# Placing the tiles of a saturated matmul kernel in SBUF by their address modulo 128 bytes

## The reference

```python
def _L0_gnn_ref(input_graph, adj, Wq, bq, Wk, bk, Wv, bv, beta):   # 12 heads of 32
    q, k, v = (_split_heads(input_graph @ W + b) for each of the three)
    scores = jnp.einsum('bhqd,bhkd->bhqk', q, k) / sqrt(32) + beta * adj_e
    scores = jnp.where(adj_e > 0, scores, -9e15)
    return merge_heads(jnp.einsum('bhqk,bhkd->bhqd', jax.nn.softmax(scores, -1), v))
# _L1_gnn_ref: two layers, each
    a = jax.nn.softmax(jnp.einsum('bid,bjd->bij', h, h) / sqrt(384), axis=-1)
    delta = a * adjacency_matrix
    attn = delta / (jnp.sum(delta, axis=-1, keepdims=True) + 1e-10)
    hl, hs, hr = h @ wl.T + b_l, h @ ws.T + b_s, h @ wr.T + b_r
    ctx = (attn * upper) @ hl + diag(attn)[..., None] * hs + (attn * lower) @ hr
    h = relu(layernorm(ctx) * g + beta)
x = _layernorm(x + _L0_gnn_ref(x, adj, ...), axis=-1)
x = _layernorm(x + _L1_gnn_ref(x, adj, ...), axis=-1)
```

## The kernel before

| | function | moving | stationary | columns moved | matmuls per step |
|---|---|---|---|---|---|
| H | `project_sides`, `project_self` | `w_hi`, `w_lo` | `hT_hi`, `hT_lo` | 384 | 108 |
| A | `mix` | `hlr_hi`, `hlr_lo` | `aT_hi`, `aT_lo` | 386 | 24 |
| V | `project_v` | `w_hi`, `w_lo` | `xT_hi`, `xT_lo` | 384 | 18 |
| Q | `project_qk` | `xT_hi`, `xT_lo` | `w_hi`, `w_lo` | 256 | 54 |

## Time and profile before

### The profile page before, as it was taken

One profiled execution on the slowest core, in us unless ns is written; L12 is line 12 of the kernel. 1 busy time (PEld: TensorE's weight loads), 2 busy tenths in 40 slices (PEclk: granted clock), 3 DMA queues, 4 the chain that ended last, 5 costly groups with the idle time before them and its releaser, 6 DMA issues.

```text
span 1405.7 us, 37486 instructions
## 1 busy us (share of the span) xinstructions
PE 1345.0 (96%) x13568; PEld 1321.4 (94%) x13568; DVE 1085.8 (77%) x2665; ACT 755.5 (54%) x1579; POOL 597.0 (42%) x656
## 2 busy tenths in 40 slices
PE   3799999999999999999999999999999999999894
PEld 3799999999999999999999999999999999999894
DVE  3358887878887888887787888788888778787765
ACT  4355555564555555555555555555555555555453
POOL 1334444444444444444444445444444444444432
PEclk9799999999999999999999999999999999999997
DMA  7210111110011111011111011111001111101000
GB/s 239 77 39 8 44 50 51 50 49 20 29 49 49 49 49 36 12 49 49 49 49 49 14 35 49 49 49 49 25 24 49 49 49 49 49 2 40 24 13 23
DMA packets 49445, 62.74 MB, mean 45 GB/s; under 512 B 14320, under 2 KB 35952, under 8 KB 49392
## 3 DMA queue, kind: packets, MB, share of 16 engines
q1 hardware_dynamic: 49392, 62.03, 14.4%
HBM read 36.44 MB, written 12.58 MB: 35 GB/s over the span
## 4 chain that ended last, share of the span: by engine, by line
PE 95%; DMA 2%; DVE 1%; issue 1%; ACT 1%; POOL 0%; SPq 0%; POOLq 0%; ACTq 0%
PE bank L315 26%; PE bank L317 25%; PE bank L316 25%; PE bank L392 5%; PE bank L426 4%; PE bank L378 3%; PE bank L364 3%; PE bank L413 2%; PE bank L403 2%; DMA late<-in_w 2%; PE bank L454 1%; ACT w_hi L519 0%; DVE ln_six L840 0%; DVE w_lo L682 0%; ACT late L620 0%
## 5 line engine op out<-in xcount | busy, mean ns | idle before, releaser
L315 PE MATMUL bank<-w_hi,hT_hi 128*128 128x384 f32 x1152 | 402.9, 350 | 4.5 <-issue 3.6
L316 PE MATMUL bank<-w_lo,hT_hi 128*128 128x384 f32 x1152 | 390.7, 339 | 0.0
L317 PE MATMUL bank<-w_hi,hT_lo 128*128 128x384 f32 x1152 | 390.7, 339 | 0.0
L996 POOL TENSOR_TENSOR hlr_lo<-late,hlr_hi 128x384 fp32r<-128x384 f32 x256 | 239.5, 941 | 264.9 <-ACT hlr_hi L595 263.1
L595 ACT ACTIVATE hlr_hi<-late 128x384 fp32r<-128x384 f32 x256 | 134.3, 524 | 212.2 <-DVE late L797 210.3
L315 PEld LDWEIGHTS bank<-w_hi,hT_hi 128*128 128x128 f32 x1152 | 216.9, 188 | 10.1 <-issue 5.7
L316 PEld LDWEIGHTS bank<-w_lo,hT_hi 128*128 128x128 f32 x1152 | 217.4, 189 | 0.0
L317 PEld LDWEIGHTS bank<-w_hi,hT_lo 128*128 128x128 f32 x1152 | 217.0, 188 | 0.0
L797 DVE TENSOR_TENSOR late<-bank,rows 128x384 f32<-128x384 f32 x256 | 141.9, 554 | 89.2 <-PE bank L317 88.5
L1009 POOL TENSOR_TENSOR ln_rstd<-ln_var,minus_half 128x2 f32<-128x2 f32 x128 | 98.9, 772 | 225.0 <-DVE ln_var L866 117.3
L315 PE MATMUL bank<-xT_hi,w_hi 128*128 128x256 f32 x576 | 164.6, 286 | 9.1 <-ACT kT L534 9.1
(11 more groups left out here) (93 smaller groups left out, 2903.2 us busy)
## 6 DMA issues: line engine op xcount, KB each, us to landing
v_halves<-v_stage SPq DMA_DIRECT2D x128, 99.0 KB, 2.3
xT_in<-in_xT SPq DMA_DIRECT2D x32, 384.0 KB, 3.2
x_in<-in_x SPq DMA_DIRECT2D x32, 384.0 KB, 3.9
out<-late SPq DMA_DIRECT2D x32, 384.0 KB, 2.4
late<-in_w SPq DMA_DIRECT2D x9, 576.0 KB, 6.2
adj_in<-in_adj SPq DMA_DIRECT2D x32, 64.0 KB, 3.6
adjT_in<-in_adjT SPq DMA_DIRECT2D x64, 32.0 KB, 2.9
rows<-in_bl SPq DMA_DIRECT2D x2, 192.0 KB, 6.2
```

Of the source, the lines that this page charges most:

```text
L315: nc.tensor.matmul(o, l_hi, r_hi, start=n == 0, stop=False)
L316: nc.tensor.matmul(o, l_hi, r_lo, start=False, stop=False)
L317: done = nc.tensor.matmul(o, l_lo, r_hi, start=False, stop=n == last)
L996: nc.gpsimd.tensor_tensor(hlr_lo[:, t, m, 0:D], hlr[:, t, m], hlr_hi[:, t, m, 0:D].bitcast(F32), ALU.subtract).then_inc(hlrlo_ready, 1)
```

## The change

The change moves tiles within SBUF and pads one kind of row. All that moves through TensorE in a large product with the weights or in `mix`, and `kT`, `ident` and `v_halves`, now starts at a multiple of 128 bytes. After `v_halves` (6336 bytes, 49.5 x 128) come the tiles that are stationary, 64 bytes behind a multiple. The small tiles that TensorE doesn't read come last. The row of `hlr_hi` and `hlr_lo` is allocated 416 floats long (`MPAD`, 1664 bytes, 13 x 128) in place of 386; the matmul still moves 386 of them. Engine for engine, every instruction, its shape, its waits and its place in the order are the same in both kernels.

```diff
+MPAD = 416
@@
         w_hi = sb("w_hi", [P, NW, KC, D], F32R)
         w_lo = sb("w_lo", [P, NW, KC, D], F32R)
+        kT = sb("kT", [P, KC, TOK])
+        ident = sb("ident", [P, P])
+        hlr_hi = sb("hlr_hi", [P, T, 2, MPAD], F32R)
+        hlr_lo = sb("hlr_lo", [P, T, 2, MPAD], F32R)
         rows = sb("rows", [P, 9, D])
-        bq_col, bk_col = sb("bq_col", [P, KC]), sb("bk_col", [P, KC])
...
+        v_halves = sb("v_halves", [P, T, GRAPHS, H * VW])
         xT_hi = sb("xT_hi", [P, KC, TOK], F32R)
         xT_lo = sb("xT_lo", [P, KC, TOK], F32R)
-        qT, kT = sb("qT", [P, KC, TOK]), sb("kT", [P, KC, TOK])
-        v_stage = sb("v_stage", [P, T, H, VW])
-        v_halves = sb("v_halves", [P, T, GRAPHS, H * VW])
...
+        qT = sb("qT", [P, KC, TOK])
+        pT = sb("pT", [P, T * PAIRS, P])
         probs = sb("probs", [P, T, HC, 2, 2, N])
...
-        hlr_hi = sb("hlr_hi", [P, T, 2, MW], F32R)
-        hlr_lo = sb("hlr_lo", [P, T, 2, MW], F32R)
...
+        bq_col, bk_col = sb("bq_col", [P, KC]), sb("bk_col", [P, KC])
...
                     product(CTX_BANKS[t][:, 0:MW],
-                            [((aT_hi[:, t, m, :], aT_lo[:, t, m, :]), (hlr_hi[:, t, m, :], hlr_lo[:, t, m, :]))
+                            [((aT_hi[:, t, m, :], aT_lo[:, t, m, :]), (hlr_hi[:, t, m, 0:MW], hlr_lo[:, t, m, 0:MW]))
```

More of the change, by code:

```diff
@@ L127, in resnorm_kernel @@
         adj_diag = sb("adj_diag", [P, 2, T, N])
+        v_halves = sb("v_halves", [P, T, GRAPHS, H * VW])
         xT_hi = sb("xT_hi", [P, KC, TOK], F32R)
         xT_lo = sb("xT_lo", [P, KC, TOK], F32R)
-        qT, kT = sb("qT", [P, KC, TOK]), sb("kT", [P, KC, TOK])
-        v_stage = sb("v_stage", [P, T, H, VW])
-        v_halves = sb("v_halves", [P, T, GRAPHS, H * VW])
-        score_mask = sb("score_mask", [P, T, N])
-        score_add = sb("score_add", [P, T, N])
+        qT = sb("qT", [P, KC, TOK])
+        pT = sb("pT", [P, T * PAIRS, P])
         probs = sb("probs", [P, T, HC, 2, 2, N])
-        row_max = sb("row_max", [P, T * H])
-        pT = sb("pT", [P, T * PAIRS, P])
-        r_sum = sb("r_sum", [P, T, H])
         h0 = sb("h0", [P, 2, T, D])
@@ L146, in resnorm_kernel @@
         hT_lo = sb("hT_lo", [P, T, KC, P], F32R)
-        u_max, u_bias = sb("u_max", [P, T]), sb("u_bias", [P, T])
         e_di = sb("e_di", [P, T, 2, N])
-        z_di = sb("z_di", [P, T])
-        diag_junk = sb("diag_junk", [P, T, N])
-        diag, dz, den, den_sq = sb("diag", [P, T]), sb("dz", [P, T]), sb("den", [P, 2, T]), sb("den_sq", [P, 2, T])
-        hlr_hi = sb("hlr_hi", [P, T, 2, MW], F32R)
-        hlr_lo = sb("hlr_lo", [P, T, 2, MW], F32R)
         aT = sb("aT", [P, T, 2, P])
@@ L166, in resnorm_kernel @@
                  for r in range(RAW)]
+        bq_col, bk_col = sb("bq_col", [P, KC]), sb("bk_col", [P, KC])
+        g0_col, b0_col = sb("g0_col", [P, KC]), sb("b0_col", [P, KC])
+        beta_col = sb("beta_col", [P, 1])
+        diag_sel = sb("diag_sel", [P, N])
+        minus_half = sb("minus_half", [P, T])
+        bv_row = rows[:, 0, :]
+        bias_row = [[rows[:, 1 + 3 * l + m, :] for m in range(3)] for l in range(2)]
+        g1_row, b1_row = rows[:, 7, :], rows[:, 8, :]
+        v_stage = sb("v_stage", [P, T, H, VW])
+        score_mask = sb("score_mask", [P, T, N])
+        score_add = sb("score_add", [P, T, N])
+        row_max = sb("row_max", [P, T * H])
+        r_sum = sb("r_sum", [P, T, H])
+        u_max, u_bias = sb("u_max", [P, T]), sb("u_bias", [P, T])
+        z_di = sb("z_di", [P, T])
+        diag_junk = sb("diag_junk", [P, T, N])
+        diag, dz, den, den_sq = sb("diag", [P, T]), sb("dz", [P, T]), sb("den", [P, 2, T]), sb("den_sq", [P, 2, T])
         def norm_tiles(name):
```

## The result

| | before | after |
|---|---|---|
| median of 20 runs each, interleaved | 1406.8 us | 1403.66 us |
| ratio after/before | | 0.9977 (95% interval 0.9970 to 0.9985) |
| span of the profiled execution | 1405.7 us | 1401.5 us |
| H: mean distance of starts in a run of 36, without its first | 176.6 ns | 173.5 ns |
| one step in the steady part (between starts of V) | 41.721 us | 41.637 us |

The kernel got faster, by about 3 us where 12 had been forecast.

What follows compares the result with a forecast made beforehand. PE was taken to bound the kernel through the distances between its matmul starts. H's 11.0 us and A's 1.2 us, all else 0, summed to 12.2 us, from 1405.5 to 1393.3 us; 8-in-10 range 1374 to 1400.

Steps and rivals of the forecast that it cites:

- H's price: Matmuls of 384 columns with `hT` tiles stationary: 176.8 to 173.5 ns each over 3328 distances, 11.0 us less.
- What differs is where the stationary operand lies: H against V: stationary operand at 32 against 64 past a multiple of 128, taken as the reason for 3.3 ns.
- A: Matmuls of 386 columns in `mix`: moving slices all at 0, 175.8 to 174.3 ns for 768, 1.2 us less.
- The waits that exist don't grow either: Other engines: the chain to layer 0's `hT_lo` keeps its length, no wait is new; priced at 0.
- Their tiles move by 32 or 64 bytes, and I price that at 0: Tiles of the engines other than PE: their new addresses cost nothing, being covered by PE.
- The sign that the prediction named: Prediction wrong if PE's waits grow by what H saves, showing as idle time ahead of L315.
- the slower case: Rival: H at 180 ns, 10.6 us more, 1416.1 us; decided by H's mean above 177.1 ns; chance 0.06.
- the fast phase: Rival: H and A settle 4.3 ns below V's price, 29.7 us less, 1375.8 us; chance 0.21.
- no change: Rival: H's gap to V comes from bank, neighbours or place in the step; 1405.5 us, chance 0.13.
- rule of two independent read ports: Skill's rule for PE's SBUF reads: no address could matter, sum 0, 1405.5 us; the prediction held the rows against it.
- The estimate of 162.5 ns for 384 columns: H by the skill's columns/2.4 + 2.5 ns: 48 us less if reached; no row came near it.
- The two prices of Q: Q at 117.6 ns behind V, 113.3 behind transposes; starting phase counts, 4.3 ns per matmul either way; Q's change priced 0.

Runs made afterwards that it cites:

- late8_w160: `after_late8` with only `w_hi` and `w_lo` moved, from 128 to 160 past a multiple of 256: 1409.92 us, ratio 1.0025.
- after_late8: The changed kernel, pad kept, with `late` (hlr, h_self, c0, c1) 8 bytes further on: 1395.99 us, ratio 0.9929 to the kernel before.
- before_h128: The kernel before with only `hT`, `hT_hi` and `hT_lo` moved 128 bytes on: 1396.68 us, ratio 0.9936.
- after_nopad: The changed kernel without its pad, rows of `hlr_hi` and `hlr_lo` at 386 floats again: 1401.23 us, ratio 0.9963 to the kernel before.
- lo8: The changed kernel with `hlr_lo` 8 bytes on; its room moves tiles behind by 128 bytes modulo 256: 1406.71 us, one run.
- pool8: `after_late8` with `xT_in` and `h0` also 8 bytes on: 1393.96 us, ratio 0.9912 to the kernel before.
- h_only: The kernel before with H's stationary operands moved to 64 past a multiple of 128, tiles behind by 128 bytes: 1397.59 us, ratio 0.9931.
- late8_h32: `after_late8` with `hT`, `hT_hi` and `hT_lo` at 32 past a multiple of 128: ratio 0.9929 to the kernel before.

## Why the prediction was wrong

H's price: the number was right. 173.5 ns was forecast and measured. A step saves (176.6 - 173.5) x 34 twice and (176.4 - 173.4) x 16 twice, 0.31 us, so 9.8 us over 32 steps for the 11.0 of the sum. The size is off by the reading of before from one run rounded to 0.01 us (176.8 for a mean of 176.6), and by 3328 distances taken where 3200 lie within the runs.

Its reason: wrong. "What differs is where the stationary operand lies: 64 bytes past a multiple of 128 in V, 32 in H" was true and not the cause. The distance between load and stream modulo 256 is: 192 for V, 160 for H. The number came out right by luck: the change happened to bring H to 192 as well.

A: mis-sized. 1.2 us was forecast; the distances within A's run went from 176.8 to 176.5 ns, which over 768 matmuls is 0.2 us. So the mixed remainders weren't what made A dear. With the pad its slices lie 1664 bytes apart, 6.5 times 256, so its distance alternates between 192 and 64; whether that matters wasn't tried.

The step that lost the gain is this one: "The waits that exist don't grow either". I had followed the chain to `hT_lo` of layer 0 alone. The chain to `mix` has `project_self` for its cover, 18 H, and what was left over was 0.23 us (from the end of `aT_lo` to the first A it was 0.58 us before, and 0.35 when PE waited for it). Its cover became shorter and its length grew by 0.42 us. It cost 234 ns a step ahead of layer 1's `mix`, and A's first distance in each layer grew from 171 to 233 ns on average, 123 ns a step: 0.36 us together, more than H had saved. About 0.10 us came back where H waits for `hT_lo` in layer 0 (from the last `gram` to the first H, 238 to 187 ns on average over both layers, so 103 a step). Together with 0.02 us in `scores` that is -0.31 + 0.36 - 0.10 - 0.02 = -0.07 us a step, and -0.084 was measured.

It began with "Their tiles move by 32 or 64 bytes, and I price that at 0". For ACT and most of DVE that was right. For POOL's subtraction it was 155 ns on every second one, and POOL's end holds DVE. The sign that the prediction named, idle time ahead of the line of the matmuls, didn't show on PE; it showed on PEld and in the distances.

Two of its readings are off without consequence. The bound of the slower case takes 1.2, which is A's saving in us, where 1.5 ns for each A belongs; it moves from 177.1 to 177.15 ns. And the 113.3 ns of Q behind transposes are read from the later part of the run, after it has settled; all distances but the first have a mean of 114.2.

The rivals: the fast phase didn't come, no change was nearest in time, though for another reason, and the slower case wasn't seen; `late8_w160` shows that the rule of 128 bytes can be kept and the kernel get slower. The Trainium skill's rule of two independent read ports (page "TensorE: Matmul & The Clock Gate", section "Step-by-step: what each phase is for") had been read in the prediction as saying that no address could matter. In that reading this case contradicts it: moving the weights alone by 32 bytes changed the distance between V's starts from 173.0 (`after_late8`) to 176.8 ns (`late8_w160`). The estimate of 162.5 ns for 384 columns took a formula that the same page, section "Back-to-back issue gap", gives for an isolated matmul and not for a stream of loads and matmuls; no run here comes below 173.0.

The two prices of Q were real. The run behind the transposes took 2.23 us in before, after, `after_late8` and `before_h128`, and 2.29 us in `after_nopad`, `lo8` and `pool8`, where its distance modulo 256 was another. But it also took 2.29 us in `h_only` and `late8_h32`, where Q's own remainders, by 256 too, were those of before. That is 0.06 us a step, 2 us in all, and what sets it in those two is open.

## What to carry to other kernels

Where an engine that is always busy gets faster, follow each chain of the other engines back from every wait on it, not only the one that waits today, and write down how long it is and what is left over. Addresses are an operand too, of every engine: before moving or padding a tile, list who else reads it and at what distance from its other input. A comparison of two groups in one trace gives a price that can be trusted and a cause that can't, until one thing alone is moved.

## What the runs showed of the hardware

- At the full clock, matmuls of 384 float32r columns follow each other every 173.0 to 173.5 ns where the stationary operand starts 192 bytes further than the moving one modulo 256, and every 176.2 to 176.8 where it starts 160 further. Both are above 160.0, half of the 320.0 at half the clock. There the distance of addresses shows nothing: 320.0 at 192, and (44.61 - 41.73)/9 = 320.0 at 160, V in `late8_w160`:

```profile
41.73 0.52 PE L318 MATMUL bank<-w_lo,xT_hi 128*128 128x384 f32 x1
...
44.61 0.42 PE L318 MATMUL bank<-w_lo,xT_hi 128*128 128x384 f32 x1
```

- GpSimd's operation on two full float32 inputs in SBUF takes 866 ns for 384 columns where their starts differ by 8 modulo 16 bytes, and 1002 to 1034 where they are equal; for 768 columns 1558 and 1853. The output's place made no difference (1016). Differences of 4 and 12 weren't tried.
- DVE's `aT_lo` ends 0.55 us behind the end of the GpSimd operation that it meets, whether it takes 0.69 us in all or 0.90.
